# Gate and up products of the expert blocks with the weights standing and x moving, h coming out transposed

## The reference

```python
gate_logits = jnp.einsum('ble,en->bln', x, gate_kernel)
top_k_weights, top_k_indices = jax.lax.top_k(gate_logits, TOP_K)
softmax_probs = jax.nn.softmax(top_k_weights.astype(jnp.float32), axis=-1)
weights = weights.at[b_idx, l_idx, top_k_indices].set(softmax_probs)
layer_w0 = jnp.einsum('ble,neh->blnh', x, w0_kernel)
layer_w1 = jnp.einsum('ble,neh->blnh', x, w1_kernel)
layer_mult = jax.nn.silu(layer_w0) * layer_w1
intermediate = jnp.einsum('blnh,nhe->blne', layer_mult, wo_kernel)
output = jnp.einsum('blne,bln->ble', intermediate, weights)
```

## Time and profile before

| what | us |
|---|---|
| median of 3 runs (lowest, highest) | 2596.48 (2596.28, 2597.36) |
| the profiled execution | 2600.14 |
| its span | 2598.3 |
| PE busy in it | 2351.5 (90%) |
| DVE, ACT, POOL busy | 1619.5, 1291.2, 1287.2 |
| stage of expert blocks, first gate product | 2172.2 |
| its last scatter starts | 2593.4 |

### The profile page before, as it was taken

One profiled execution on the slowest core, in us unless ns is written; L12 is line 12 of the kernel. 1 busy time (PEld: TensorE's weight loads), 2 busy tenths in 40 slices (PEclk: granted clock), 3 DMA queues, 4 the chain that ended last, 5 costly groups with the idle time before them and its releaser, 6 DMA issues. The chain is left out here.

```text
span 2598.3 us, 43352 instructions
## 1 busy us (share of the span) xinstructions
PE 2351.5 (90%) x13283; PEld 1445.1 (56%) x13299; DVE 1619.5 (62%) x3299; ACT 1291.2 (50%) x2555; POOL 1287.2 (50%) x2086
## 2 busy tenths in 40 slices
PE   6997999999996977999999999889869966999998
PEld 4665886666663653445344453456646653666665
DVE  5996774655556966877768777489967653212111
ACT  4774544444443982666565667557743421222222
POOL 3675771334443652334343535458865224666663
PEclk8998999999998997999999999899989987999999
DMA  4001000000100014131231311000013151322222
GB/s 144 6 1 70 0 0 1 1 1 1 49 1 17 1 34 104 32 96 41 63 86 32 103 50 50 25 25 26 1 51 129 41 205 30 47 45 47 45 45 33
DMA packets 86132, 115.41 MB, mean 44 GB/s; under 512 B 15480, under 2 KB 65536, under 8 KB 84272
## 3 DMA queue, kind: packets, MB, share of 16 engines
q1 hardware_dynamic: 67408, 92.65, 11.9%
q0 software_dynamic: 18528, 20.31, 5.0%
HBM read 78.01 MB, written 34.64 MB: 43 GB/s over the span
## 5 line engine op out<-in xcount | busy, mean ns | idle before, releaser
L3768 ACT ACTIVATE L2S_pT<-L2S_t_ps 128x512 f32<-128x512 f32 (+3 forms) x768 | 356.4, 491 | 224.2 <-PE L2S_t_ps L3589 215.7
L3832 DVE TENSOR_REDUCE L2S_mx<-L2S_s_ps 128x1 f32<-128x768 f32 (+7 forms) x384 | 350.4, 951 | 105.5 <-PE L2S_s_ps L3512 104.8
L3589 PE MATMUL L2S_t_ps<-L2S_q,L2S_k 98*128 98x512 bf16 (+3 forms) x768 | 250.3, 337 | 17.2 <-DMA L2S_q<-L2S_mrow 6.5
L4074 POOL TENSOR_SCALAR_AFFINE_SELECT L2S_pT<-L2S_pT 128x128 f32<-128x128 f32 x512 | 151.0, 309 | 177.4 <-ACT L2S_pT L3768 172.9
L3511 PE MATMUL L2S_s_ps<-L2S_k,L2S_q 96*128 96x512 bf16 (+3 forms) x768 | 202.1, 336 | 10.9 <-DVE L2S_mx L3832 6.9
L646 POOL TENSOR_TENSOR L_prob<-L_prob,L_rc 128x616 f32<-128x616 f32 x64 | 82.2, 1285 | 231.5 <-DVE L_rc L570 231.5
L4451 DVE TENSOR_TENSOR L3B_h<-L3B_si,L3B_u_ps 128x512 f32<-128x512 f32 x71 | 48.8, 688 | 236.9 <-PE L3B_u_ps L4394 236.9
L3589 PEld LDWEIGHTS L2S_t_ps<-L2S_q,L2S_k 98*128 98x128 bf16 x768 | 73.3, 98 | 198.1 <-ACT L2S_pT L3768 127.8
L4368 POOL DMA_INDIRECT out<-L3B_y,L3F_rows x71 | 114.7, 1616 | 134.6 <-DVE L3B_y L4457 109.4
L3689 PE MATMUL L2S_o_ps<-L2S_pT,L2S_v 128*32 128x512 f32 (+3 forms) x1536 | 167.3, 509 | 0.0
L321 PE MATMUL L_scores<-weights,L_xT 128*128 128x308 f32 x512 | 143.2, 423 | 2.3 <-ACT L_xT L444 1.6
(11 more groups left out here) (553 smaller groups left out, 5700.9 us busy)
## 6 DMA issues: line engine op xcount, KB each, us to landing
qk_parts<-L2S_part SPq DMA_DIRECT2D x84, 128.0 KB, 2.4
L2S_q<-qk_parts SPq DMA_DIRECT2D x32, 192.0 KB, 3.4
L2S_k<-qk_parts SPq DMA_DIRECT2D x30, 192.0 KB, 3.4
L2S_q<-qk_parts SPq DMA_DIRECT2D x32, 128.0 KB, 3.2
L3F_w<-in_L_gu SPq DMA_DIRECT2D x8, 512.0 KB, 8.1
weights<-in_L_w SPq DMA_DIRECT2D x8, 512.0 KB, 9.7
out<-x_sb SPq DMA_DIRECT2D x8, 512.0 KB, 3.3
expert_rows<-L_xn SPq DMA_DIRECT2D x8, 512.0 KB, 3.6
```

The costliest lines, as they stand in the source:

```text
L3589: nc.tensor.matmul(o[:, lo:512], k6[:, q % 2, j, kt * P:(kt + 1) * P], q6[:, q % 2, c, j, lo:512], start=True, stop=True).then_inc(s["t_fu ...
L3768: nc.scalar.activation(pT[:, st % SLOTS, j, lo:512], t_ps[j % 2][:, lo:512], ACT.Exp, scale=SK).then_inc(s["exp_done"], 1)
L3832: nc.vector.tensor_reduce(dst, src, AX.X, ALU.max).then_inc(s["mx_done"], 1)
L4074: nc.gpsimd.affine_select(out=edge, in_=edge, compare_op=ALU.is_ge, fill=0.0, base=0, pattern=[[1, P]], channel_multiplier=-1).then_inc(s[ ...
```

## The change

Gate and up are turned round. The expert's weights now stand, in pieces of 128 by 128 (four chunks of the 512 columns, two chunks of features), and `xT` moves, 128 columns of tokens. Each piece of 128 columns of g and u comes out with features on partitions, which is what `down` needs standing. So `turn_h`, `copy_h`, `hT_ps`, `hT` and their semaphores go, and the pipeline has one phase less.

The standing weights are not addressed by the register. A new phase of DVE, `fetch`, reads the expert number, and copies the block's part of w0 and w1 (128 by 1024 elements of fp32 each) into one of two buffers `own` in `chip.arena`, at a fixed address. It runs one phase ahead of `up`, which waits for it through `own_done`; the register read in `up` goes. `fetch` waits until the `up` two blocks earlier is done with the buffer. `mul` writes `h` after the down product of two blocks before (it waited for the turn of h).

```diff
@@ -4335,12 +4335,14 @@
             return ctx.enter_context(nc.psum_tensor(f"L3B_{name}", shape, F32))
 
         g_ps, u_ps = [ps(f"g_ps{i}", [P, F]) for i in range(2)], [ps(f"u_ps{i}", [P, F]) for i in range(2)]
-        xT_ps, hT_ps = ps("xT_ps", [P, 512]), ps("hT_ps", [P, 512])
+        xT_ps = ps("xT_ps", [P, 512])
         o_ps = [ps(f"o_ps{i}", [P, 512]) for i in range(2)]
         xb, xT, y = sb("xb", [P, AHEAD, D]), sb("xT", [P, 2, KD, P]), sb("y", [P, AHEAD, D])
         share = sb("share", [P, 2 * AHEAD])
-        si, h, hT = sb("si", [P, 2, F]), sb("h", [P, 2, F]), sb("hT", [P, 2, FK, P])
-        names = "xT_full xT_free g_full u_full si_done h_done hT_full hT_free o_full y_done".split()
+        si, h = sb("si", [P, 2, FK, P]), sb("h", [P, 2, FK, P])
+        at = KD * E * F
+        own = chip.arena[:, at:at + 4 * KD * F].rearrange("p (b m k n) -> p b m k n", b=2, m=2, k=KD)
+        names = "xT_full xT_free own_done g_full u_full si_done h_done o_full y_done".split()
         s = {n: ctx.enter_context(nc.semaphore(f"L3B_{n}")) for n in names}
         loaded, added = [chip.queued[f"gathered{q}"] for q in range(AHEAD)], chip.queued["scattered0"]
         block = ctx.enter_context(nc.Block(no_gpsimd_drain=True))
@@ -4387,35 +4389,28 @@
             def up(j, q):
                 pe.wait_ge(s["xT_free"], j + 2)
                 pe.wait_ge(s["h_done"], j + 1)
-                chip.settle(pe)
-                e = pe.value_load(table[0:1, bass.ds(j, 1)], min_val=0, max_val=E - 1)
-                for o, wt, done in ((g_ps, w0, "g_full"), (u_ps, w1, "u_full")):
-                    for k in range(KD):
-                        mm = nc.tensor.matmul(o[q % 2][:], xT[:, q % 2, k, :], wt[:, k, bass.ds(e * F, F)], start=(k == 0), stop=(k == KD - 1))
+                pe.wait_ge(s["own_done"], j + 1)
+                for o, m, done in ((g_ps, 0, "g_full"), (u_ps, 1, "u_full")):
+                    for c in range(FK):
+                        for k in range(KD):
+                            mm = nc.tensor.matmul(o[q % 2][:, c * P:(c + 1) * P], own[:, q % 2, m, k, c * P:(c + 1) * P], xT[:, q % 2, k, :],
+                                                  start=(k == 0), stop=(k == KD - 1))
                     mm.then_inc(s[done], 1)
 
-            def turn_h(j, q):
+            def down(j, q):
                 pe.wait_ge(s["h_done"], j + 3)
-                pe.wait_ge(s["hT_free"], j + 1)
-                for k in range(FK):
-                    mm = nc.tensor.transpose(hT_ps[:, k * P:(k + 1) * P], h[:, q % 2, k * P:(k + 1) * P], chip.ident[:])
-                mm.then_inc(s["hT_full"], 1)
-
-            def down(j, q):
-                pe.wait_ge(s["hT_free"], j + 2)
                 pe.wait_ge(s["y_done"], j + 1)
                 chip.settle(pe)
                 e = pe.value_load(table[0:1, bass.ds(j, 1)], min_val=0, max_val=E - 1)
                 for k in range(FK):
-                    mm = nc.tensor.matmul(o_ps[q % 2][:, 0:D], hT[:, q % 2, k, :], wo[:, k, bass.ds(e * D, D)], start=(k == 0), stop=(k == FK - 1))
+                    mm = nc.tensor.matmul(o_ps[q % 2][:, 0:D], h[:, q % 2, k, :], wo[:, k, bass.ds(e * D, D)], start=(k == 0), stop=(k == FK - 1))
                 mm.then_inc(s["o_full"], 1)
 
-            run(pe, [none, turn_x, up, turn_h, down, none])
+            run(pe, [none, turn_x, up, down, none])
 
         @block.scalar
         def _(act):
             act.sem_inc(s["xT_free"], 1)
-            act.sem_inc(s["hT_free"], 1)
 
             def copy_x(j, q):
                 act.wait_ge(s["xT_full"], j + 1)
@@ -4427,28 +4422,31 @@
             def gate(j, q):
                 act.wait_ge(s["g_full"], j + 1)
                 act.wait_ge(s["h_done"], j + 1)
-                nc.scalar.activation(si[:, q % 2, :], g_ps[q % 2][:], ACT.Silu).then_inc(s["si_done"], 1)
-
-            def copy_h(j, q):
-                act.wait_ge(s["hT_full"], j + 1)
-                if not (isinstance(j, int) and j < 2):
-                    act.wait_ge(s["o_full"], j - 1)
-                nc.scalar.activation(hT[:, q % 2, :, :].rearrange("p k t -> p (k t)"), hT_ps[:], ACT.Copy).then_inc(s["hT_free"], 1)
-
-            run(act, [none, copy_x, gate, copy_h, none, none])
+                nc.scalar.activation(si[:, q % 2].rearrange("p c t -> p (c t)"), g_ps[q % 2][:], ACT.Silu).then_inc(s["si_done"], 1)
+
+            run(act, [none, copy_x, gate, none, none])
 
         @block.vector
         def _(dve):
             dve.sem_inc(s["h_done"], 2)
             dve.sem_inc(s["y_done"], 2)
 
+            def fetch(j, q):
+                if not (isinstance(j, int) and j < 2):
+                    dve.wait_ge(s["u_full"], j - 1)
+                chip.settle(dve)
+                e = dve.value_load(table[0:1, bass.ds(j, 1)], min_val=0, max_val=E - 1)
+                nc.vector.tensor_copy(own[:, q % 2, 0], w0[:, :, bass.ds(e * F, F)])
+                nc.vector.tensor_copy(own[:, q % 2, 1], w1[:, :, bass.ds(e * F, F)]).then_inc(s["own_done"], 1)
+
             def mul(j, q):
                 dve.wait_ge(s["si_done"], j + 1)
                 dve.wait_ge(s["u_full"], j + 1)
 
                 if not (isinstance(j, int) and j < 2):
-                    dve.wait_ge(s["hT_full"], j - 1)
-                nc.vector.tensor_tensor(h[:, q % 2, :], si[:, q % 2, :], u_ps[q % 2][:], ALU.mult).then_inc(s["h_done"], 1)
+                    dve.wait_ge(s["o_full"], j - 1)
+                nc.vector.tensor_tensor(h[:, q % 2].rearrange("p c t -> p (c t)"), si[:, q % 2].rearrange("p c t -> p (c t)"), u_ps[q % 2][:],
+                                        ALU.mult).then_inc(s["h_done"], 1)
 
             def result(j, q):
                 dve.wait_ge(s["o_full"], j + 1)
@@ -4456,7 +4454,7 @@
                     dve.wait_ge(added, (j - AHEAD + 1) * 16)
                 nc.vector.tensor_scalar(y[:, q % AHEAD, :], o_ps[q % 2][:, 0:D], share[:, q:q + 1], None, ALU.mult).then_inc(s["y_done"], 1)
 
-            run(dve, [none, none, mul, none, result, none])
+            run(dve, [none, fetch, mul, result, none])
 def clear_semaphores(nc):
 
     with nc.Block(no_gpsimd_drain=True) as block:
```

## The result

The changed kernel takes 2580.02 us (median of 4 runs, 2575.85 to 2581.6), the kernel before beside it 2596.92 (4 runs): 16.9 us less, ratio 0.9917 with a 95% interval of 0.9903 to 0.9932. The forecast was faster, 2573.5 us. The result lies in the stated range (2568 to 2600), though 1 us above the narrower one that the forecast itself was given (2569 to 2579). The profiled execution took 2581.6 us around a span of 2579.9.

What follows compares the result with a forecast made beforehand. TensorE was taken to bound the expert blocks: 0.29 us less per block, 23.7 less up to result 68, 0.7 back, net 23.0, so 2577.1 us profiled and 2573.5 median; range 2568 to 2600, narrower 2569 to 2579.

Steps and rivals of the forecast that it cites:

- PE is the bound: Expert blocks: TensorE busy every microsecond at full clock, so its time sets the pace; block 5.82 us before, 5.53 after.
- Gate and up at 0.112 us per record: Gate and up: 32 records of 128 columns, each with new weights, take 3.58 us against 3.44, a loss of 0.14.
- The rival on weight loads: Gate and up: 32 unhidden loads of 0.19 us make a block 8.0 us, kernel 2755; chance 0.05, shared with the sequencer.
- Turning h, down and the sequencer: TensorE per block: turning h goes, 0.43 us; down keeps 1.73; expert-number read priced at nothing, 0.6 us without cover.
- The copies: VectorE's two weight copies per block: 0.66 us each, 1.32 together, hidden within the 5.53 us block.
- The two ends: Pipeline's end: result 68 comes 23.7 us earlier, scatter 69 waits 5.3 us for its result, giving 0.7 back; net 23.0.
- GpSimd as the bound: Rival: copies cost GpSimd up to 1.32 us per block against 0.75 slack; chances 0.13 below old pace, 0.12 slower.
- The 4.78 us of the earlier trace: GpSimd's shortest round, scatter to scatter, read where it catches up; left 0.75 us of slack against 5.53.
- Two signs: GpSimd in the forecast: copies meet the scatter; its idle time stands ahead of the scatter, still ended by `y`.

Runs made afterwards that it cites:

- e4: Changed kernel with four 128x128 transposes put back ahead of the down product, into a spare bank; 2611.38 us, 1.0035 of the kernel before.
- e5: Changed kernel with each gate and up product cut into two of 64 moving columns, each with its own weight load; 2846.14 us, ratio 1.0931.
- e2: Changed kernel without VectorE's weight copies, every block computed with expert 0's weights at a fixed place; 2581.03 us, 0.9911 of the kernel before.
- e3: Kernel before plus VectorE's weight copies and TensorE's wait for them, products untouched; 2603.25 us, ratio 1.0002.
- e6: Changed kernel with VectorE also copying both weight pieces into scrap buffers; 2580.43 us, 0.9917 of the kernel before.
- e7: Changed kernel with the weight copies on ScalarE, behind its copy of x, instead of VectorE; 2577.55 us, 0.9904 of the kernel before.
- e10: Changed kernel with TensorE's first turn of x waiting until the fourth block's rows have landed; 2583.98 us, one run.
- e11: Changed kernel with one more GpSimd memset of 128x1024 per block, between gathers and scatter; 2584.01 us, 0.9940 of the kernel before.
- e9: Changed kernel with 20 extra 128x128 TensorE products at the stage's start and 8 behind the first turn of x; 2580.05 us, ratio 0.9922.
- e12: e8 with GpSimd's gathers of blocks 4 to 7 waiting for the up product four blocks before; 2573.76 us, 0.9898 of the kernel before.
- e1: Changed kernel run again, unaltered; 2577.07 us, 0.9909 of the kernel before.
- e8: Changed kernel with four extra 128x512 TensorE products at the stage's start and two behind the first turn of x; 2581.54 us, ratio 0.9922.

## Why the prediction was right

**PE is the bound: right.** e4 put 0.43 us of PE per block back and got all of it (30.3 us of 30.5).

**Gate and up at 0.112 us per record: the number right, the reason beside it half right.** The prediction said that most of a load hides behind the columns. e5 shows that it is the other way about: a floor per record with new weights sets the 0.112 us, most likely the load, and 128 columns just fit beneath it. From the earlier trace rows 128 columns are a quarter of 0.43, 0.107 us, so the edit loses only 0.005 us per record. The rival on weight loads priced them at 0.19 us, the duration that the profile lists; its price was wrong, though its mechanism is probably the one at work.

**Turning h, down and the sequencer: right.** 0.44 us in e4, 1.72 us for down, and no idle time ahead of it in steady blocks. Once, at the first down product, the sequencer's read stood uncovered, and the gap was 1.14 us rather than the 0.6 that the prediction named for that case.

**The copies: right.** Listed at 0.70 us on the mean (0.66 forecast), 0.61 from start to start, and hidden: e2, e3, e6 and e7 all show nothing in the time.

**The two ends: a term was missing.** Result 69 came 5.30 us after result 68, as forecast. But the sum treated the start of the stage as unchanged but for one gate-and-up and turn. In the profiled executions 4.5 us are missing (2581.6 against the forecast 2577.1). The late signals took some 2.3 of them (two gaps of PE, 1.13 and 1.14); e10 without them has 402.6 us against 405.5. Another 2.6 us lie ahead of the stage (cast at 2165.0 rather than 2162.4), and these come and go from run to run; 0.4 came back between cast and first gate product (9.4 us, before 9.8). The median is 6.5 us above the forecast of 2573.5: the other 2 us come from the 3.7 by which the profiled execution was taken to lie above the median, where it now lay 1.6. So the pace of the blocks was forecast, and the nearness of the total depended on chance too.

**GpSimd as the bound: its condition never came near.** The loss was 0.18 us per block (e2 against the changed kernel), not up to 1.32, and the room was larger than 0.75: e11 puts 0.975 us on top and the pace holds. The 4.78 us of the earlier trace rows contained a wait of 0.59 us ahead of the scatter, so as POOL's shortest round it was too long. Two signs came otherwise than forecast: the copies met the gathers, not the scatter, and POOL's idle time stood ahead of the gather, ended by the turn of x (66.8 us in 62 blocks), not ahead of the scatter, ended by `y`.
The Trainium skill (SBUF — State Buffer, section Who interferes with whom) lets a two-port DVE copy block GpSimd for its whole length. In the block shown the copies (2421.57 to 2422.88) lie over the two gathers for about 1 us, and on the mean POOL lost 0.18 us; so the measurement bears out a hold-up, at a fifth of the length that the rule names.

**What the late signals are stays open.** They don't belong to the new products alone, nor to the copies alone: they come with the new products without copies (e2) and with the copies beside the old products (e3, 3 us late), and not in the kernel before. Shown is further that they come longer with more PE instructions ahead (e9), and are gone when POOL's unbroken row of gathers is out of the way (e10), spread out (e11) or, nearly, cut short (e12). In the changed kernel, e1 to e4, e6 and e7 ACT's first late copy starts 1.9 to 2.1 us after that row of gathers ended (2184.44 and 2182.40 in the changed kernel), at whatever record PE had stopped; since POOL stops because it waits for a late signal itself, this alone doesn't say which causes which. Not shown is the path on which the two meet, nor whether the recording of an execution has a part in it, since every stage length here comes from a recorded one.
The Trainium skill (NOTIFIC — the notification-queue block, section Overflow: three behaviours, one of which stalls the engine) says that the block through which engines write their records can hold an engine up when an internal queue fills. A delay that grows with the instructions of PE (e9) and comes with more of DVE's as well (e3) would fit; no run here can show it.

## What to carry to other kernels

Where a product's result is only turned afterwards, look whether swapping the standing and the moving operand gives it turned: the price is one weight load per 128 columns, and in fp32 that was 0.005 us per record here, since the floor of a record with new weights (0.112 us) is about what 128 columns take (0.107). Going below 128 moving columns saved nothing here: a record kept its 0.112 us with 64. When an edit shortens a late stage, compare that stage from its own first instruction, not the whole time, and look at its first two blocks by themselves.

## What was not expected of the hardware

- A record of 64 moving columns with new weights costs as much as one of 128: 0.112 us at full clock and 0.21 at half (e5).
- With those 64-column records the clock stayed at half for 31 us although PE had work all the time; the changed kernel's rose 3.8 us after its first gate product (2174.4, 2178.2). The stretches of e5, in the columns of the earlier trace rows behind the length:

```profile
2174.00:2188.00 14.00, 14.00 (x68) 14.00 (x67) 0.02 (x1) 2.26 (x3) 6.51 (x7) 0.50 0.14 38
2188.00:2205.00 17.00, 17.00 (x74) 16.33 (x73) 2.65 (x4) 0.98 (x2) 2.22 (x2) 0.50 0.03 9
2205.00:2212.00 7.00, 7.00 (x58) 6.85 (x56) 1.78 (x3) 0.98 (x2) 3.76 (x3) 0.90 0.14 25
```

- Signals of PE that reach other engines 3 to 7 us after the product is over, in the first blocks alone (the changed kernel, e3, e8, e9; 2.8 us in e5).
